# Feed-forward activations turned by VectorE in squares of 32 by 32, and the next output projection one step sooner

## The reference

```python
x = layernorm(x + attention(x))            # 16 query heads, 4 key heads of 16, rotary, full softmax, then @ wo
x = layernorm(x + ffn(x))

# ffn, with W = (int - 128) * scale; 256 -> 1024 -> 256
g = einsum('bsh,ih->bsi', x, Wg)
u = einsum('bsh,ih->bsi', x, Wu)
h = silu(g) * u
return einsum('bsi,hi->bsh', h, Wd)
```

## Time and profile before

| | |
|---|---|
| median of 3 runs | 938.3 us (937.12 to 938.52) |
| the profiled execution's own time | 940.06 us |
| its span, first to last instruction | 938.2 us |
| TensorE busy | 918.4 us, 98% |
| VectorE busy | 754.3 us, 80% |
| ScalarE busy | 715.2 us, 76% |
| GpSimd busy | 249.0 us, 27% |
| mean granted TensorE clock | 0.982 |

### The profile page before, as it was taken

How to read it: one execution, slowest core, us unless ns; L and a number is a source line. 1 busy time by engine, 2 the same in 40 slices (tenths; PEclk the granted TensorE clock), 3 DMA queues, 4 the chain that set the end, 5 groups by cost and what they waited for, 6 DMA issues and landing times.

```text
span 938.2 us, 15754 instructions
## 1 busy us (share of the span) xinstructions
PE 918.4 (98%) x5566; PEld 467.3 (50%) x5566; DVE 754.3 (80%) x1518; ACT 715.2 (76%) x930; POOL 249.0 (27%) x213
## 2 busy tenths in 40 slices
PE   9998999999999999999999999999999999999995
PEld 3323444343434343434444344434335888888884
DVE  5677999999999999999999999999974456655544
ACT  1446888998898988889988989898896555555563
POOL 6753556010010001001000100400101766666444
PEclk9986999999999999999999999999999999999997
DMA  7986433322132232223313123221110201110001
GB/s 240 283 220 184 109 92 75 76 73 58 42 74 67 47 69 64 50 59 74 71 42 76 45 64 69 70 50 43 32 53 15 68 24 45 46 37 31 23 23 47
DMA packets 50081, 68.79 MB, mean 73 GB/s; under 512 B 13521, under 2 KB 23761, under 8 KB 50001
## 3 DMA queue, kind: packets, MB, share of 16 engines
q1 hardware_dynamic: 49136, 64.61, 27.0%
q0 software_dynamic: 864, 3.15, 1.0%
HBM read 46.74 MB, written 16.25 MB: 67 GB/s over the span
## 4 chain that ended last, share of the span: by engine, by line
PE 90%; DVE 3%; ACT 2%; issue 2%; POOL 1%; DMA 1%; SPq 1%; POOLq 0%; DVEq 0%; ACTq 0%
PE pv_bank L1241 27%; PE ring_bank L1148 26%; PE pair_bank L1299 13%; PE pair_bank L1362 12%; PE pv_bank L1371 3%; PE ring_bank L1371 3%; PE ring_bank L1251 2%; PE pair_bank L1189 1%; ACT probs L1072 1%; PE ring_bank L1161 1%; POOL rotated L540 1%; PE ring_bank L1266 1%; PE pv_bank L1130 1%; DMA q_parts<-low 0%; DVE by_sin L720 0%
## 5 line engine op out<-in xcount | busy, mean ns | idle before, releaser
L1072 ACT ACTIVATE probs<-pair_bank 128x1024 f32<-128x1024 f32 x512 | 496.5, 1027 | 68.8 <-PE pair_bank L1299 67.5
L755 DVE TENSOR_REDUCE block_max<-ring_bank 128x1 f32<-128x512 f32 x732 | 469.0, 682 | 32.1 <-PE ring_bank L1148 24.4
L1148 PE MATMUL ring_bank<-k_max,q_sb 48*128 48x512 f32 x1003 | 315.9, 477 | 3.5 <-DMA q_sb<-q_parts 1.5
L1241 PE MATMUL pv_bank<-probs,v_all 128*32 128x512 f32 x2048 | 273.7, 606 | 0.6 <-ACT probs L1072 0.5
L1148 PEld LDWEIGHTS ring_bank<-k_max,q_sb 48*128 48x128 f32 x1003 | 136.9, 185 | 252.4 <-DVE block_max L755 125.8
L1299 PE MATMUL pair_bank<-q_sb,k_sb 50*128 50x512 f32 x1024 | 204.8, 416 | 0.9 <-ACT probs L1072 0.7
L618 POOL TENSOR_TENSOR attn<-attn,inv_rows 128x1024 f32<-128x1024 f32 x7 | 16.7, 2380 | 491.2 <-DMA inv_rows<-inv_d 491.2
L1299 PEld LDWEIGHTS pair_bank<-q_sb,k_sb 50*128 50x128 f32 x1024 | 101.6, 187 | 33.2 <-ACT probs L1072 14.4
L929 DVE SCALAR_TENSOR_TENSOR hid<-pair_bank,up_s,silu 128x512 f32<-128x512 f32 x64 | 47.9, 748 | 86.8 <-ACT silu L1112 86.8
L660 POOL TENSOR_TENSOR hid_l<-hid,hid_h 128x512 fp32r<-128x512 f32 x64 | 82.9, 1295 | 87.7 <-ACT hid_h L1098 86.9
L752 DVE CUSTOM_DVE_ANT_0 above<-ring_bank,above 128x512 f32<-128x512 f32 x137 | 94.4, 691 | 13.3 <-ACT above L1017 5.2
(11 more groups left out here) (128 smaller groups left out, 857.9 us busy)
## 6 DMA issues: line engine op xcount, KB each, us to landing
k_max<-k_parts SPq DMA_DIRECT2D x96, 96.0 KB, 3.5
q_sb<-q_parts SPq DMA_DIRECT2D x64, 128.0 KB, 3.4
k_sb<-k_parts SPq DMA_DIRECT2D x96, 64.0 KB, 2.4
attn<-xT SPq DMA_DIRECT2D x8, 512.0 KB, 4.9
q_parts<-high SPq DMA_DIRECT2D x16, 256.0 KB, 3.8
q_parts<-low SPq DMA_DIRECT2D x16, 256.0 KB, 3.9
q_sb<-q_parts SPq DMA_DIRECT2D x64, 64.0 KB, 3.6
attn<-pv_sb SPq DMA_DIRECT2D x128, 32.0 KB
```

The costliest lines, as they stand in the source:

```text
L755: dve.reduce_max(block_max[half % 2][:, col:col + 1], bank, axis=AX.X).then_inc(ring_used, 1)
L1072: act.activation(probs[t % 2][:, 2 * pr:2 * pr + 2, :], pair_bank[pr][:], ACT.Exp, scale=D ** -0.5).then_inc(probs_ready, 1)
L1148: pe.matmul(bank, q_sb[k][rows, i, qt * P:(qt + 1) * P], k_max[k // QH][rows, kind * CH:(kind + 1) * CH], start=True, stop=True).then_inc( ...
L1241: ins = pe.matmul(pv_bank[32 * j:32 * j + 2 * D, :], v_all[:, head, t, :], probs[t % 2][:, 2 * (j % 2) + j // 2, :], start=(t == 0), stop= ...
```

## The change

In the blocks 1 to 7 the turning of x1 moves from TensorE to VectorE. VectorE's transpose turns squares of 32 by 32. One instruction reads 32 partitions of x1 (a group q of 32 tokens, 8 squares: 4 tiles t by 2 tiles k, 256 elements a partition) and writes 32 partitions of x1T (a group j of 32 features); 4 x 4 of them turn a block. They are issued behind hid of step 4 (q = 0, 1) and of step 5 (q = 2, 3), and wait for all of x1. x1T is no longer in PSUM: it lies in SBUF, over the two pv_sb buffers, so that the first block waits for the last DMAs from there. The cast and the split of x1T read it from SBUF and move from step 6 to step 7.

The next block's output projection goes from step 1 to step 0, where it stands between the down products of steps 0 and 1, and waits for the residual sums of the block before instead of x1T_l. The chain between is moved along: residual and statistics to step 0, the first norm's rsqrt to step 1 on GpSimd, its application on ScalarE to step 3, and add_x1 and the second norm's statistics to steps 2 and 3. The aggregation stays in step 1.

```diff
+SQ = 32
...
+        pv_both = sb("pv_both", [P, QH, CH])
+        pv_sb = [pv_both[:, c, :] for c in range(QH)]
...
+        x1T = pv_both
...
-                        if it == 2 and not (last and c == 1):
+                        if it == 1 and not (last and c == 1):
                             rsqrt1(m + 1)
...
+            def turn_squares(m, c, q):
+
+                dve.wait_ge(x1_ready, TT * m + TT)
+                if m == 1 and q == 0:
+                    for half in range(QH):
+                        dve.wait_ge(attn_stored[half], 2 * STORES * PAIRS)
+                for j in range(P // SQ):
+                    dst = x1T[j * SQ:(j + 1) * SQ].rearrange("p k (t q a) -> p q t k a", t=TT, a=SQ)[:, q]
+                    src = x1[c][q * SQ:(q + 1) * SQ].rearrange("p t (k j i) -> p j t k i", k=KE, i=SQ)[:, j]
+                    dve.transpose(dst, src).then_inc(squares_turned, 1)
+
             def split_x1T(m, c):
                 for k in range(KE):
                     dve.wait_ge(x1T_h_ready, 2 * m + k + 1)
-                    dve.tensor_tensor(x1T_l[c][:, k, :], ring_bank[k][:], x1T_h[c][:, k, :].bitcast(fp32), ALU.subtract).then_inc(x1T_l_ready, 1)
+                    dve.tensor_tensor(x1T_l[c][:, k, :], x1T[:, k, :], x1T_h[c][:, k, :].bitcast(fp32), ALU.subtract).then_inc(x1T_l_ready, 1)
...
-                        if it == 6 and nxt:
+                        if it == 7 and nxt:
                             split_x1T(m + 1, 1 - c)
...
-                        if it == 1 and nxt:
+                        if it == 0 and nxt:
                             add_residual(m + 1, 1 - c)
                             norm1_stats(m + 1, 1 - c)
+                        if it == 1 and nxt:
                             norm1_aggregate(m + 1)
+                        if it in (4, 5) and nxt:
+                            turn_squares(m + 1, 1 - c, 2 * (it - 4))
+                            turn_squares(m + 1, 1 - c, 2 * (it - 4) + 1)
+                        if it == 2 and prev:
+                            add_x1(m - 1, 1 - c)
                         if it == 3 and prev:
-                            add_x1(m - 1, 1 - c)
-                        if it == 4 and prev:
                             norm2_stats(m - 1, 1 - c)
                             norm2_aggregate(m - 1)
...
             def split_x1T(m, c):
                 for k in range(KE):
-                    act.wait_ge(x1T_ready, 2 * m + k + 1)
-                    act.activation(x1T_h[c][:, k, :], ring_bank[k][:], ACT.Copy).then_inc(x1T_h_ready, 1)
+                    act.wait_ge(squares_turned, (P // SQ) ** 2 * m)
+                    act.activation(x1T_h[c][:, k, :], x1T[:, k, :], ACT.Copy).then_inc(x1T_h_ready, 1)
...
-                        if it == 6 and not (last and c == 1):
+                        if it == 7 and not (last and c == 1):
                             split_x1T(m + 1, 1 - c)
...
-                        if it == 4 and not (last and c == 1):
+                        if it == 3 and not (last and c == 1):
                             norm1_apply(m + 1, 1 - c)
...
-                    pe.wait_ge(x1T_l_ready, 2 * m - 1 + h)
+                    pe.wait_ge(res_added, 2 * m - 1 + h)
                     project_part(m, c, h, 0, 12)
...
-                                if it == LAG - 1 and not (last and c == 1):
+                                if it == 0 and not (last and c == 1):
                                     project_out(m + 1, 1 - c)
...
-                            if it == 5 and not (last and c == 1):
-                                transpose_x1(m + 1, 1 - c)
```

More of the change, by code:

```diff
@@ L113, in layer @@
         any_low, no_low = sb("any_low", [1, 1]), sb("no_low", [1, 1], i32)
-        pv_sb = [sb(f"pv_sb{c}", [P, CH]) for c in range(QH)]
+        pv_both = sb("pv_both", [P, QH, CH])
+        pv_sb = [pv_both[:, c, :] for c in range(QH)]
         stats = sb("stats", [P, TT, 6])
@@ L197, in layer @@
         x1T_ready, x1T_h_ready, x1T_l_ready = sem("x1T_ready"), sem("x1T_h_ready"), sem("x1T_l_ready")
+        squares_turned = sem("squares_turned")
         gu_ready, silu_ready, hid_ready, hid_h_ready, hid_l_ready = sem("gu_ready"), sem("silu_ready"), sem("hid_ready"), sem("hid_h_ready"), sem("hid_l_ready")
```

## The result

| | before | after |
|---|---|---|
| median | 938.3 us | 970.6 us (966.7 to 975.4, 5 runs) |
| ratio | | 1.034 (95% interval 1.032 to 1.037) |
| profiled execution, its span | 940.06, 938.2 | 966.70, 964.8 |
| mean granted clock of it | 0.982 | 0.979 |
| first gate matmul of block 0 | 718.56 | 714.52 |

A forecast was written before the change was run, and what follows sets the result against it. TensorE's work was taken to bound the kernel; squares on VectorE would outlast it. Six blocks +13.3, block 0 +4.67 and block 7 +0.1 make +18.1 on the median 938.3: 956.4 us, range 943 to 970.

The forecast's parts named there:

- The bound: Blocks 1 to 6 before the change: time is the sum of TensorE's work, which has no slack; 26.35 a block.
- The chain of a block: Changed blocks: norm, hid products, 16 squares at s each and splits let the next block start at 21.45 + 16 s.
- The projection one step sooner: Blocks 1 to 6: step 2's down product waits for the scaling of the sum banks, 0.34 a block.
- The squares are held: VectorE: each square changes the written partitions, so it waits until the one before has ended; all 16 held.
- rival (a): Squares on VectorE are not held and start 0.333 apart, giving 943.9; 14%.
- Block 0: First block: residual and statistics delay hid(1), and GpSimd's rsqrt delays a low part; block 1 starts 4.67 later.
- Rival (c): Squares need what GpSimd's operations hold and wait for them: 26 more, about 980; 7%.
- The price of a square: VectorE's transposes, 16 a block: 0.445 start to start, bounds 0.333 and 0.56, from ordinary 256-element operations.
- The second norm's steps, one sooner, fill idle time of VectorE.: Changed blocks: these moved steps fit in VectorE's idle third of each window, so no cost was added.
- The granted clock unchanged.: Changed profile: TensorE's granted clock was expected to stay as before, listed among the signs to be seen.
- The estimate beside it, 0.475: Square's start to start time by the Trainium skill's 311 ns for 128 bf16 elements, put on 256; sum 959.8.
- rival (d): Not slower: a square takes at most 0.273, about 936.8; 7% faster, 6% for near 0.28, within 0.2%.

The follow-up runs named there:

- e1: The changed kernel with VectorE's sum of feed-forward output and x1 cut from 1024 columns to 2; 967.0 us, its one block with a fast head 28.90.
- e5: The changed kernel with GpSimd's second copy and split of the attention rows in step 3, not step 1; median 959.8 us.
- e10: The changed kernel with GpSimd's second copy and split in step 3 and 20 unread matmuls ahead of TensorE's wait for x1T_l; median 957.0 us.
- e8: The changed kernel with later copy and split, scaling ahead of hid(1), squares 2, 7, 7 in steps 3 to 5, second norm's statistics in step 7; 957.2 us (1.020).
- e3: The changed kernel with each square written to the partitions it is read from, so x1T is wrong; 950.4 us (1.0125).

## Why the prediction was wrong

What held:

- The bound. TensorE had no slack, and the turn of x1 became the chain. Blocks are 25.79 without the squares' wait (25.82 predicted).
- The chain of a block. With the measured 0.466 it gives 21.45 + 16 x 0.466 = 28.91, and the one block of e1 that has neither the long split nor a slow head is 28.90.
- The projection one step sooner costs 0.32 a block (0.34), by the wait it named.
- The squares are held: 0.466 start to start, 0.33 when the partitions stay. The rule of the Trainium skill (page "VectorE: DVE Perf Modes", section "Two Vector instructions with no wait between them") agrees with both numbers; rival (a) falls.
- Block 0 lasts 29.90, predicted 29.81. Part of this is luck: with 0.466 the sum would have been 30.15.
- Rival (c) falls: squares ran at 0.43 to 0.44 next to GpSimd's operations, and their group has no long ones.

What failed, by its step:

1. **The price of a square**, a term mis-sized: 0.445 taken, 0.466 measured (436 ns and 0.03). That is 0.34 a block, 2.4 in all. The 436 ns are 21 above the 415 of an ordinary operation of 256 elements, but it is not shown that the turning costs them: squares that keep their partitions start 0.33 apart, as those ordinary operations do, and last 0.39. The estimate beside it, 0.475, was nearer.
2. **"The second norm's steps, one sooner, fill idle time of VectorE."** This edit was costed at nothing by looking at VectorE alone. The sum of y and x1 has both inputs in SBUF, moved into the time of GpSimd's split, and the split then lasts 2.38. The longer split costs 29.95 - 28.90 = 1.05 a block (e1), in blocks 1 to 5 5.3 in all. (With rsqrt taken out from behind the split as well, e5, it is 29.95 - 28.57 = 1.38, but the other 0.33 was in the prediction's chain.) The earlier trace rows had shown a VectorE operation of 4 elements lasting 0.96, to the end of GpSimd's split. The prediction used them for the squares, as rival (c), and did not ask the same of the operations that it moved. The Trainium skill, page "SBUF — State Buffer", section "SBUF: two separate sides", says it as a rule: a VectorE operation with two SBUF inputs and a GpSimd operation that reads SBUF take a port pair from each other for a whole instruction. The traces agree on the split: 2.38 against 1.31. By the recorded spans they do not on rsqrt ahead of the sum, 1.01 and 1.22 with 0.8 of overlap.
3. **"The granted clock unchanged."** It stood in the list of what would be seen, with no term of the sum and no rival. Behind the wait that the prediction itself put at the head of each block (2.7, measured 2.4) the clock was at 1.2 GHz in some of them: 1.5 each, four or 6.0 in the traced execution, 7.5 in the median by the kernel with the 20 matmuls.

The median: 956.4 + 2.4 - 0.3 + 5.3 + 7.5 = 971.3, or 969.8 with the 6.0 of the trace; measured 970.6. (The -0.3 is block 6, which has no copy and split ahead of its rsqrt, so that its squares began sooner than I had them.) The traced execution: 956.3 + 2.1 + 5.3 + 4 x 1.5 = 969.7, less 4.0 for its earlier start, 965.7; measured 964.8. The 0.9 between them: block 0 is 0.25 shorter than with dearer squares (29.90, not 30.15), and from the start of block 7 to the end it is about 0.5 less than predicted.

That e10, without the second and third term, comes to 28.57 a block and 957.0, next to the 28.57 and 956.4 of the prediction, is luck in part. It holds the dearer squares, 0.34 a block; as much is made up for by the norm, which starts sooner there than in the prediction, since rsqrt is no longer behind the second copy and split. Block 0 is shorter too (28.15, not 29.81). The confirmation of the prediction's chain is the 28.90 of e1.

The range was too narrow for the same reason. Its upper end, 970, was the unit price of a square at its bound, and it held no term for what a long wait brings with it or for what the moved steps meet.

What stays open: when exactly a wait at the head leads to a slow start. Idle times of the same 2.4 did both, in one execution, and so did 1.95 in e8 (three slow of seven). With 1.5 in e3 no head was slow. Open too is how many slow heads the executions without a trace had, and so how the 7.5 divides into heads and chance.

Two slips of the recorded sums change nothing: block 0's +4.67 is 4.63 by its own terms, and rival (d)'s terms add up to -1.2.

## What to carry to other kernels

Where a step moves, look at what the other engine sharing its port does at the new time, not only at whether its own engine is idle there. Where a new wait of TensorE comes out of the sum, ask next what the wait does to its clock, and put a price on it: here the slow starts cost 6.0 in the trace and 7.5 by the medians, which 20 useless matmuls a block gave back. And before work is taken from a busy engine, compare its price on both: 0.87 of TensorE's time a block became 7.5 of VectorE's, in a chain that had some 4 to spare.

## What was not expected of the hardware

- STREAM_TRANSPOSE on 32 partitions by 256 fp32 elements lasts 436 ns; successive ones start 0.466 apart when the written partitions change, 0.33 when they stay (e3, where they last 0.39).
- A VectorE sum of 1024 elements with both inputs in SBUF and GpSimd's operations held each other up in both directions: 1.29 became 2.38, 1.01 became 1.99, 1.21 became 1.96. It depends on the order: an rsqrt that was recorded 0.2 ahead of the sum left both at 1.01 and 1.22. The squares, 0.43 to 0.44 beside GpSimd's operations, were not lengthened.
- After 2.4 of idle time TensorE's clock was at 1.2 GHz at some heads and at 2.4 GHz at others of one execution. Half of the spread of equal kernels, 966.7 to 975.4, can come from there; the kernel before, without such waits, spreads from 935.5 to 944.6 over all its runs.
